# Relative-position attention with a mixture of experts: rows of maxima in one transfer, near values loaded later, routing steps and two small blocks moved to other slots

## The chip, the cores and the metric

The kernel runs on 1 core of one Trainium2 chip (trn2). The metric is device microseconds of one execution. Before: 1708.11 us, the median of 3 runs (1687.08 to 1716.86).

## The reference

x is [4, 1024, 128] in float32. The output is x + attention(xn) + ffn(xn), with xn the layer norm of x. The attention has 16 heads of 8 numbers, with a learned bias by distance (63 buckets, clipped at 31) on the queries and on the keys, and a term by distance on the values:

```python
attn = jnp.einsum('bhid,bhjd->bhij', q, k)                 # q scaled by hd ** -0.5
attn = attn + take_along_axis(einsum('bhid,hdm->bhim', q, rpe_k_table), idx)
attn = attn + swapaxes(take_along_axis(einsum('bhjd,hdm->bhjm', k * scale, rpe_q_table), idx), 2, 3)
attn = jax.nn.softmax(attn, axis=-1)
out = jnp.einsum('bhij,bhjd->bhid', attn, v)
S = segment_sum(attn over j, by bucket of i and j)         # 63 sums for each i
out = out + jnp.einsum('inbh,hnd->bhid', S, rpe_v_table)
x_out @ w_proj.T + b_proj
```

The ffn is a routed one (64 experts, the 6 best of a softmax for each of 4096 tokens, at most 64 tokens for an expert) beside a shared one.

## The kernel before

The attention is worked off head by head: 4 batches x 16 heads are 64 "heads", numbered 0 to 63. Each engine has its own hand-written program. They all run through iterations h, and an iteration has 16 slots s. In a slot TensorE makes two score tiles of 128 x 512, with small pieces around them:

- the first unit, of head h + 1, from Q1 and K1 (banks 0 and 1). VectorE reads it for the maxima of its rows (`tops`, line 1622). The bank is free again when VectorE has read it, so the first unit of slot s waits for the read of slot s - 2;
- the second unit, of head h - 1 in slots 0 to 5 and of head h from slot 6 on (LAG = 6), from Q2 and K2 (banks 2 and 3). Rows 8 to 10 of Q2 (ROW_M) hold the negated maxima in three bf16 parts, so that the scores come out with the maximum taken off, and ScalarE takes the exponential into PT (line 1277);
- in odd slots the product with the values; in slot 4 the query side of the distance bias for head h + 4 (copied by ScalarE into dq_e, line 1307, written to memory by SP, read back sheared as dq_s); in slot 7 its key side; in slot 13 the near values, a product of the windows WP with TOE. TOE depends on the attention head alone and is loaded by SP once for two heads (line 504), in odd iterations h (and once more after the experts).

Between the two passes over a head stand the maxima. VectorE folds `tops` into `top` (line 1603) in slot 0, TensorE transposes it in slot 1 (line 981), VectorE reduces the result and cuts it into three bf16 parts (lines 1611 to 1618, on 32 partitions, with a semaphore behind each operation), and SP copies the parts into the three rows of Q2, one transfer for a row (line 512). TensorE asks for them at slot 6, with `own(mrow_in, 48 * (h + 1))` (line 887).

SP's order in an iteration: TOE (if due), the maxima, rows of Q1 and K1 for head h + 2, dq_d, rows of Q2 and K2 for h + 1, operands of slots 4 and 7, the source of the windows (aj_d), and dq_s. All of these are issued from one queue. ScalarE issues the loads of the windows WT from its own queue, in slots 1, 5, 9 and 13. In slot 4 it copies a finished output of head h - 2 out of a bank (Oev, line 1332).

The routing for the experts runs on VectorE beside the heads: `routing(h)` gives q, j = divmod(h + 3, 7) for q < 4, and in the iterations with j of 3 to 6 (16 of them, heads 0 to 24) four "listing" steps find the best tokens of an expert one after another (`dve.max` on 576 columns, line 1537, and `match_replace`, line 1539). After head 29 the experts are computed, then the loop goes on with heads 30 to 63.

## Time and profile before

| | |
|---|---|
| median of 3 runs | 1708.11 us |
| profiled execution | 1702.14 us, span 1700.3 us |
| TensorE busy | 1428.5 us (84%) |
| VectorE busy | 1140.3 us (67%) |
| ScalarE busy | 797.6 us (47%) |
| GpSimd busy | 542.0 us (32%) |
| mean granted clock of TensorE | 0.864 |
| DMA | 289.55 MB, 170 GB/s |

The chain that ended last has TensorE for 52% of the span, VectorE for 23%, DMA for 8% and SP's queue for 6%. The page gives, for each group of instructions, the busy time and the idle time of its engine just before it with what ended that; the same can be asked for any stretch of time. The profile writes SPq for instructions of SP's queue, and x3 for three of a kind in a row.

### The profile page before, as it was taken

How to read it: one execution, taken by the hardware profiler on the slowest of the kernel's cores; microseconds unless marked ns; L12 is line 12 of the kernel's file. 1: busy time of each engine (PE TensorE's matmuls, PEld its weight loads, DVE VectorE, ACT ScalarE, POOL GpSimd, SP SyncE). 2: the span in 40 equal slices, each digit the busy share in tenths (PEclk: the TensorE clock that was granted, in tenths of full speed). 3: DMA queues.
4: the chain of work that ended last, by engine and by line, in shares of the span. 5: the costliest groups of instructions: out<-in, count | busy, mean ns of one | idle time of the engine just before them, and what ended most of it. 6: DMA issues, size and time to landing. Idle time of an engine off the chain costs nothing.

```text
span 1700.3 us, 67734 instructions
## 1 busy us (share of the span) xinstructions
PE 1428.5 (84%) x29626; PEld 963.5 (57%) x29626; DVE 1140.3 (67%) x2468; ACT 797.6 (47%) x1408; POOL 542.0 (32%) x555
## 2 busy tenths in 40 slices
PE   3376498888988989888889998989988888898897
PEld 1233255555655556555558666666656665666665
DVE  7275467878787786867653466777766666656672
ACT  2133134555455454544442255555545554545454
POOL 2244212222222222211333133444433333433343
PEclk9788558999799797977985589999989997979799
DMA  3665655776566565555555467667757665666553
GB/s 87 134 171 148 178 177 168 214 216 199 151 193 201 159 180 172 161 150 158 173 177 147 133 178 192 189 186 205 201 164 198 177 185 165 182 172 186 151 140 93
DMA packets 264392, 289.55 MB, mean 170 GB/s; under 512 B 45289, under 2 KB 195938, under 8 KB 264272
## 3 DMA queue, kind: packets, MB, share of 16 engines
q1 hardware_dynamic: 150400, 230.92, 45.0%
q10 hardware_dynamic: 102400, 50.35, 12.4%
q0 software_dynamic: 11472, 6.83, 2.8%
q8 instruction: 57, 0.93, 0.2%
q14 instruction: 63, 0.52, 0.1%
HBM read 173.84 MB, written 116.43 MB: 171 GB/s over the span
## 4 chain that ended last, share of the span: by engine, by line
PE 52%; DVE 23%; DMA 8%; SPq 6%; issue 5%; DVEq 2%; ACT 2%; POOL 1%; ACTq 1%; another core or an unknown queue 0%; POOLq 0%
PE PS L727 45%; DVE tops L1622 12%; DMA Q<-mparts 6%; PE PS L1086 5%; DVE dq_s L1648 3%; SPq L512 1%; SPq L432 1%; SPq L399 1%; DVE top L1603 1%; DVEq L1601 1%; ACT PT L1277 1%; DVE KT L1539 1%; DVE Ym L1653 1%; PE PS L1074 1%; DMA dq_s<-dq_d 1%
## 5 line engine op out<-in xcount | busy, mean ns | idle before, releaser
L1622 DVE TRANSPOSE_TENSOR_REDUCE tops<-PS 128x16 f32<-128x512 f32 x1024 | 699.7, 702 | 301.9 <-PE PS L727 295.7
L727 PE MATMUL PS<-Q,K 65*32 65x512 bf16 (+26 forms) x11904 | 722.7, 340 | 142.8 <-DVE tops L1622 73.8
L1277 ACT ACTIVATE PT<-PS 128x512 f32<-128x512 f32 x1024 | 594.6, 598 | 523.4 <-PE PS L727 470.8
L727 PEld LDWEIGHTS PS<-Q,K 65*32 65x32 bf16 (+1 forms) x11904 | 335.3, 102 | 354.7 <-DVE tops L1622 125.0
L668 POOL COPY WP<-PT 128x768 f32<-128x768 f32 x128 | 105.3, 823 | 841.5 <-PE PS L727 827.4
L727 PE MATMUL PS<-PT,Vst 128*9 128x256 f32 (+7 forms) x7552 | 366.8, 302 | 0.5 <-ACT PT L1277 0.5
L727 PE MATMUL PS<-WT,eye 96*32 96x96 bf16 (+2 forms) x4352 | 302.4, 213 | 4.6 <-DMA WT<-aj_d 3.3
L727 PEld LDWEIGHTS PS<-PT,Vst 128*9 128x9 f32 x7552 | 185.0, 95 | 72.6 <-issue 28.6
L727 PEld LDWEIGHTS PS<-WT,eye 96*32 96x32 bf16 x4352 | 190.4, 103 | 31.7 <-issue 7.2
L687 POOL TENSOR_TENSOR ajp<-dq_s,ajp 128x508 bf16<-128x508 f32 x128 | 148.8, 1163 | 10.4
L1312 ACT ACTIVATE ajp<-PS 128x508 bf16<-128x508 f32 x128 | 76.7, 599 | 88.1 <-PE PS L727 88.1
L685 POOL CAST ajp<-dq_s 128x508 bf16<-128x508 f32 x128 | 81.6, 637 | 111.5 <-DVE dq_s L1648 111.5
L727 PE MATMUL PS<-WP,TOE 128*64 128x64 f32 (+1 forms) x3072 | 115.2, 237 | 1.5 <-issue 1.5
L727 PEld LDWEIGHTS PS<-WP,TOE 128*64 128x64 f32 x3072 | 106.1, 150 | 18.2 <-issue 18.2
L656 POOL DMA_INDIRECT acc_d<-XNA,tok_i x64 | 100.8, 1575 | 42.8 <-DMA acc_d<-XNA,tok_i 36.5
L1086 PE MATMUL PS<-ident,dq_s 127*128 127x127 f32 x512 | 101.8, 333 | 14.7 <-DMA dq_s<-dq_d 14.7
L1307 ACT ACTIVATE dq_e<-PS 128x1024 f32<-128x1024 f32 x64 | 65.5, 1023 | 87.9 <-PE PS L727 87.9
L1648 DVE TENSOR_TENSOR dq_s<-PS,ajp 128x508 f32<-128x508 f32 x128 | 83.2, 650 | 28.1 <-ACT ajp L1312 28.1
L1653 DVE TENSOR_TENSOR Ym<-PS,ymask 128x512 f32<-128x512 f32 x64 | 44.3, 691 | 79.0 <-PE PS L727 70.3
L727 PE MATMUL PS<-PT,WT 128*88 128x512 f32 (+2 forms) x128 | 55.8, 630 | 44.8 <-ACT TOE L1234 29.5
L1086 PEld LDWEIGHTS PS<-ident,dq_s 127*128 127x128 f32 x512 | 68.7, 171 | 34.3 <-issue 34.3
L727 PE MATMUL PS<-tabk,Ka 71*128 71x127 bf16 x512 | 61.9, 256 | 0.0
(205 smaller groups left out, 1056.4 us busy)
## 6 DMA issues: line engine op xcount, KB each, us to landing
aj_d<-ajp SPq DMA_DIRECT2D x256, 192.0 KB
WT<-aj_d ACTq DMA_DIRECT2D x256, 192.0 KB, 3.0
dq_d<-dq_e SPq DMA_DIRECT2D x64, 512.0 KB, 4.0
dq_s<-dq_d SPq DMA_DIRECT2D x64, 512.0 KB
TOE<-toe_d SPq DMA_DIRECT2D x33, 768.0 KB
Q<-q_img SPq DMA_DIRECT2D x128, 120.0 KB, 2.6
K<-k_img SPq DMA_DIRECT2D x128, 120.0 KB, 2.7
q_img<-PT SPq DMA_DIRECT2D x48, 128.0 KB, 2.4
```

Source lines behind the costliest of these rows:

```text
L656: pool.indirect_dma_start(out=acc_d, out_offset=bass.IndirectOffsetOnAxis(ap=tok_i[:, 1 + half, n:n + 1], axis=0), in_=Y[:, n, :], in_offs ...
L668: pool.tensor_copy(WP[:, 4 * part:4 * part + 4, :], src).then_inc(win_in[part], 1)
L685: pool.tensor_copy(low[:, 0], r1).then_inc(aj_mid, 1)
L687: pool.tensor_tensor(low[:, 1], r1, low[:, 0], ALU.subtract).then_inc(aj_parts, 1)
L727: return pe.matmul(o, l, r, start=start, stop=stop, skip_group_check=True)
L1086: pe.matmul(PS[:, bank, a * P:a * P + DIST], dq_s[0:DIST, J * P:(J + 1) * P], ident[0:DIST, 0:DIST], start=a == 0, stop=False, is_transpos ...
L1277: act.activation(PT[:, TILE + N * J + 512 * half:TILE + N * J + 512 * half + 512], PS[:, 2 + u % 2, :], ACT.Exp).then_inc(s2_read, 1)
L1307: act.activation(dq_e[:, :], MISC, ACT.Copy).then_inc(dq_copied, 1)
L1312: act.activation(ajp[:, 0, 4 * part:4 * part + 4, 0:DIST], PS[:, 6 + part, :].rearrange("p (a n) -> p a n", n=P)[:, :, 0:DIST], ACT.Copy). ...
L1622: dve.tensor_reduce(tops[:, (h + 1) % 2, s // 2, 16 * (s % 2):16 * (s % 2) + 16], PS[:, s % 2, :].rearrange("p (c i) -> p c i", i=TILE), A ...
L1648: dve.tensor_tensor(dst, src, ajp[:, 0, 4 * part:4 * part + 4, 0:DIST], ALU.subtract).then_inc(aj_copied, 1)
L1653: dve.tensor_tensor(Ym[:, :].rearrange("p (m x) -> p m x", x=8), PS[:, 6, :].rearrange("p (m x) -> p m x", x=8), ymask[:, :].unsqueeze(1). ...
```

## The change

It has five parts.

1. The three parts of the maxima lie on 96 partitions, one below another (`mparts`, [3 x 32, 32]), and go into the three rows of Q2 in one transfer. Its semaphore counts 16 where it counted 48.
2. On SP the load of TOE stands behind the maxima and the rows of Q1 and K1, where it stood first.
3. On VectorE the operations on the maxima stand behind slot 1's tile, and are five where they were six: two reductions of the same columns (float32 and bf16), and three subtractions. One semaphore wait stands among them where there were four.
4. On ScalarE, Oev is copied in slot 2, where it was slot 4.
5. The listing steps stand in slots 3, 5, 6 and 7, where they stood in 5, 10, 12 and 15.

```diff
+LISTING = (3, 5, 6, 7)
...
-        mx = sb("mx", [TILE, 3, TILE])
-        mparts = sb("mparts", [TILE, 3, TILE], BF16)
+        mx = sb("mx", [2 * TILE, TILE])
+        mparts = sb("mparts", [3 * TILE, TILE], BF16)
...
                 on = lambda n: (not peeled) or 0 <= c + n < HEADS
+                if h == hm:
+                    load_distances(h + 3)
+                if on(0):
+
+                    sp.wait_ge(mparts_ready, h + 1)
+                    sp.dma_start(Q2[ROW_M:ROW_M + 3, h % PAIR, :].rearrange("p (c j) -> p c j", j=TILE),
+                                 mparts[:, :]).then_inc(mrow_in, 16)
+                if on(2):
+                    if h + 1 >= 0:
+                        sp.wait_ge(s1_ready, SLOTS * (h + 1) + 1)
+                    load_rows(h + 2, Q1, K1, rows1_in)
                 if on(-1) and fresh(h - 1):
                     wait(sp, y_psum, h - 1)
                     own = toe_d[bass.ds(place(h - 1)[1], 1), 0:SPAN, :].rearrange("a v d -> a (v d)")
                     sp.dma_start(TOE[:, :, :].rearrange("p a b -> p (a b)"),
                                  rows(own, own.offset, [[HD, P], [1, SPAN * HD]])).then_inc(toe_in, 16)
-                if h == hm:
-                    load_distances(h + 3)
-                if on(0):
-
-                    sp.wait_ge(mparts_ready, h + 1)
-                    for n in range(3):
-                        sp.dma_start(Q2[ROW_M + n:ROW_M + n + 1, h % PAIR, :].rearrange("p (c j) -> p c j", j=TILE),
-                                     mparts[:, n, :]).then_inc(mrow_in, 16)
-                if on(2):
-                    if h + 1 >= 0:
-                        sp.wait_ge(s1_ready, SLOTS * (h + 1) + 1)
-                    load_rows(h + 2, Q1, K1, rows1_in)
...
-                    own(mrow_in, 48 * (h + 1))
+                    own(mrow_in, 16 * (h + 1))
...
-                    if s == 4 and on(-2):
+                    if s == 2 and on(-2):
                         act.wait_ge(rel_done, h - 1)
                         act.wait_ge(fin_psum, h - 1)
...
-                if s in (5, 10, 12, 15) and 3 <= j:
-                    r, replace = divmod(4 * (j - 3) + (5, 10, 12, 15).index(s), 2)
+                if s in LISTING and 3 <= j:
+                    r, replace = divmod(4 * (j - 3) + LISTING.index(s), 2)
...
-                    if s == 1 and on(0):
-
-                        def hstep(ins, m):
-                            ins.then_inc(max_step, 1)
-                            dve.wait_ge(max_step, 4 * h + m)
-                        dve.wait_ge(top_psum, h + 1)
-                        wait(dve, s2_ready, SLOTS * (h - 1) + 1)
-                        dve.tensor_reduce(mx[:, 0, :], PS[0:TILE, 6, 0:P].rearrange("p (g j) -> p j g", g=4), AX.X, ALU.max,
-                                          negate=True).then_inc(top_read, 1)
-                        dve.drain()
-                        hstep(dve.tensor_copy(mparts[:, 0, :], mx[:, 0, :]), 1)
-                        hstep(dve.tensor_tensor(mx[:, 1, :], mx[:, 0, :], mparts[:, 0, :], ALU.subtract), 2)
-                        hstep(dve.tensor_copy(mparts[:, 1, :], mx[:, 1, :]), 3)
-                        hstep(dve.tensor_tensor(mx[:, 2, :], mx[:, 1, :], mparts[:, 1, :], ALU.subtract), 4)
-                        dve.tensor_copy(mparts[:, 2, :], mx[:, 2, :]).then_inc(mparts_ready, 1)
                     if on(1):
 
                         dve.wait_ge(s1_ready, SLOTS * (h + 1) + s + 1)
                         dve.tensor_reduce(tops[:, (h + 1) % 2, s // 2, 16 * (s % 2):16 * (s % 2) + 16],
                                           PS[:, s % 2, :].rearrange("p (c i) -> p c i", i=TILE), AX.X, ALU.max,
                                           apply_transpose=True).then_inc(s1_read, 1)
+                    if s == 1 and on(0):
+
+                        whole, rest = slice(0, TILE), slice(TILE, 2 * TILE)
+                        columns = PS[0:TILE, 6, 0:P].rearrange("p (g j) -> p j g", g=4)
+                        dve.wait_ge(top_psum, h + 1)
+                        wait(dve, s2_ready, SLOTS * (h - 1) + 1)
+                        dve.tensor_reduce(mx[whole, :], columns, AX.X, ALU.max, negate=True)
+                        dve.tensor_reduce(mparts[whole, :], columns, AX.X, ALU.max, negate=True).then_inc(top_read, 1)
+                        dve.drain()
+                        dve.tensor_tensor(mx[rest, :], mx[whole, :], mparts[whole, :], ALU.subtract)
+                        dve.tensor_tensor(mparts[rest, :], mx[whole, :], mparts[whole, :], ALU.subtract).then_inc(max_step, 1)
+                        dve.wait_ge(max_step, h + 1)
+                        dve.tensor_tensor(mparts[2 * TILE:3 * TILE, :], mx[rest, :], mparts[rest, :],
+                                          ALU.subtract).then_inc(mparts_ready, 1)
```

The instructions in SP's queue around the maxima, in the odd iteration h = 7 (TOE due), before:

```order
L553 DMA aj_d<-ajp 32x3x1024 x4
L493 DMA dq_s<-dq_d 128x1024
L504 DMA TOE<-toe_d 128x1536
L512 DMA Q2<-mparts 1x32x32 x3
L470 DMA Q1<-q_img 60x1024
L471 DMA K1<-k_img 60x1024
L521 DMA dq_d<-dq_e 128x1024
```

And now:

```order
L553 DMA aj_d<-ajp 32x3x1024 x4
L494 DMA dq_s<-dq_d 128x1024
L507 DMA Q2<-mparts 3x32x32
L471 DMA Q1<-q_img 60x1024
L472 DMA K1<-k_img 60x1024
L516 DMA TOE<-toe_d 128x1536
L521 DMA dq_d<-dq_e 128x1024
```

TOE has moved past three rows, and the maxima are one instruction.

On VectorE, the first half of iteration h = 8, one with listing steps (L1603 is `top`, slot 0; L1622 is a tile's read, L1607 in the kernel after; L1537 and L1539 are listing steps), before:

```order
L1603 TENSOR_REDUCE top<-tops 128x32
L1622 TENSOR_REDUCE tops<-PS 128x16
L1611 TENSOR_REDUCE mx<-PS 32x32
L1614 CAST mparts<-mx 32x32
L1615 TENSOR_TENSOR mx<-mx,mparts 32x32
L1616 CAST mparts<-mx 32x32
L1617 TENSOR_TENSOR mx<-mx,mparts 32x32
L1618 CAST mparts<-mx 32x32
L1622 TENSOR_REDUCE tops<-PS 128x16 x4
L1631 TENSOR_TENSOR Vst<-VR,TV 128x16x8
L1622 TENSOR_REDUCE tops<-PS 128x16
L1537 MAX lists<-KT 128x8
```

And now:

```order
L1603 TENSOR_REDUCE top<-tops 128x32
L1607 TENSOR_REDUCE tops<-PS 128x16 x2
L1616 TENSOR_REDUCE mx<-PS 32x32
L1617 TENSOR_REDUCE mparts<-PS 32x32
L1619 TENSOR_TENSOR mx<-mx,mparts 32x32
L1620 TENSOR_TENSOR mparts<-mx,mparts 32x32
L1622 TENSOR_TENSOR mparts<-mx,mparts 32x32
L1607 TENSOR_REDUCE tops<-PS 128x16 x2
L1537 MAX lists<-KT 128x8
L1607 TENSOR_REDUCE tops<-PS 128x16
L1630 TENSOR_TENSOR Vst<-VR,TV 128x16x8
L1607 TENSOR_REDUCE tops<-PS 128x16
```

Slot 1's tile stands ahead of the operations on the maxima, and the first listing step has come to slot 3.

The end of the same iteration, from slot 12's tile to the next `top`, before:

```order
L1622 TENSOR_REDUCE tops<-PS 128x16
L1537 MAX lists<-KT 128x8
L1622 TENSOR_REDUCE tops<-PS 128x16
L1653 TENSOR_TENSOR Ym<-PS,ymask 128x512
L1622 TENSOR_REDUCE tops<-PS 128x16 x2
L1539 MATCH_REPLACE KT<-lists,KT 128x576
L1603 TENSOR_REDUCE top<-tops 128x32
```

And now, from slot 11's small operations on:

```order
L1636 RECIPROCAL rden<-PS 128x8
L1640 TENSOR_TENSOR VR<-PS,rden 128x8x8
L1607 TENSOR_REDUCE tops<-PS 128x16 x2
L1652 TENSOR_TENSOR Ym<-PS,ymask 128x512
L1607 TENSOR_REDUCE tops<-PS 128x16 x2
L1603 TENSOR_REDUCE top<-tops 128x32
```

The two listing steps of slots 12 and 15 are gone from there.

## Rows read from the trace of the kernel before

**Rows 1.** The page's part 2: TensorE's granted clock in 40 slices of the span.

```profile
PEclk9788558999799797977985589999989997979799
```

**Rows 2.** Stretches: start:end length, busy us of PE, PEld, DVE, ACT, POOL; clock.

```profile
990.46:1608.45 617.99, 551.58 (x13033) 385.11 (x13026) 420.00 (x841) 328.52 (x581) 239.48 (x232) 0.92 0.66 184
...
1111.82:1133.94 22.12, 19.14 (x458) 13.42 (x452) 14.39 (x29) 11.34 (x20) 8.26 (x8) 0.92 0.67 193
1133.94:1153.09 19.15, 17.68 (x460) 12.48 (x454) 14.35 (x29) 11.21 (x20) 8.26 (x8) 1.00 0.67 179
1230.38:1256.82 26.44, 23.15 (x456) 15.03 (x452) 14.93 (x29) 11.57 (x20) 8.25 (x8) 0.74 0.69 192
```

**Rows 3.** TensorE's waits (us, times, longest): 990.46 to 1608.45, then 720 to 870.

```profile
PE PS L727 <- DMA Q<-mparts: 30.5, 14, 3.2
...
PE PS L727 <- DMA Q<-mparts: 7.2, 2, 4.4
```

**Rows 4.** The page's part 6: DMA issues, KB each, median us to landing.

```profile
TOE<-toe_d SPq DMA_DIRECT2D x33, 768.0 KB
Q<-q_img SPq DMA_DIRECT2D x128, 120.0 KB, 2.6
```

**Rows 5.** SP's timeline (start us, us) in heads 37 and 38.

```profile
1111.85 0.61 SPq L504 DMA_DIRECT2D TOE<-toe_d  x1
1114.34 1.79 SPq L512 DMA_DIRECT2D Q<-mparts  x3
...
1136.47 1.78 SPq L512 DMA_DIRECT2D Q<-mparts  x3
```

**Rows 6.** TensorE's timeline, [idle before]: head 38, slots 3 and 6; head 37.

```profile
1137.12 0.62 PE L727 MATMUL PS<-Q,K 65*32 65x512 bf16 x12 [0.69 <-DVE tops L1622]
1140.94 0.41 PE L727 MATMUL PS<-Q,K 65*32 65x512 bf16 x6 [0.39 <-ACT PT L1277]
...
1120.60 0.41 PE L727 MATMUL PS<-Q,K 65*32 65x512 bf16 x6 [2.11 <-DMA Q<-mparts]
```

**Rows 7.** VectorE's timeline at the start of head 38.

```profile
1135.11 0.24 DVE L1611 TENSOR_REDUCE mx<-PS 32x32 f32<-32x128 f32 x1
...
1136.28 0.17 DVE L1618 CAST mparts<-mx 32x32 bf16<-32x32 f32 x1
1136.37 1.92 DVE L1622 TRANSPOSE_TENSOR_REDUCE tops<-PS 128x16 f32<-128x512 f32 x3
```

**Rows 8.** ScalarE's timeline, slots 3 to 5 of head 38.

```profile
1138.05 0.60 ACT L1277 ACTIVATE PT<-PS 128x512 f32<-128x512 f32 x1 [0.97 <-PE PS L727]
1139.29 1.02 ACT L1307 ACTIVATE dq_e<-PS 128x1024 f32<-128x1024 f32 x1 [0.64 <-PE PS L727]
...
1140.68 0.39 ACT L1332 ACTIVATE Oev<-PS 128x256 f32<-128x256 f32 x1
```

**Rows 9.** SP's timeline in the preparation: two issues in a row.

```profile
31.15 0.28 SPq L429 DMA_DIRECT2D toe_d<-Ym  x1
31.47 22.23 SPq L432 DMA_DIRECT2D dq_d<-PT  x1
```

**Rows 10.** Head 8: a listing step; TensorE's waits for tile 11, for `top`.

```profile
411.82 0.74 DVE L1539 MATCH_REPLACE8 KT<-lists,KT 128x576 f32<-128x576 f32 x1
...
407.46 0.41 PE L727 MATMUL PS<-Q,K 71*32 71x224 bf16 x8 [0.57 <-DVE tops L1622]
...
413.31 0.29 PE L981 MATMUL PS<-ident,top 128*32 128x128 f32 x1 [0.73 <-DVE top L1603]
```

**Rows 11.** VectorE's waits in head 38, 1136 to 1145 us.

```profile
DVE tops L1622 <- PE PS L727: 3.0, 5, 1.9
```

**Rows 12.** Stretches, as in rows 2: head 8; head 10; heads 23 to 28.

```profile
392.47:412.66 20.19, 17.45 (x449) 11.79 (x449) 17.23 (x36) 11.37 (x21) 5.12 (x7) 1.00 0.62 176
...
432.84:461.20 28.36, 27.01 (x435) 17.40 (x439) 17.05 (x35) 11.64 (x20) 4.68 (x6) 0.58 0.55 162
...
720.57:869.89 149.32, 129.27 (x2698) 84.02 (x2698) 98.64 (x217) 69.31 (x122) 36.70 (x43) 0.82 0.55 159
```

More of the change, by code:

```diff
@@ L1029, in iteration @@
                         if s == 14:
-                            take(ins, mrow_in, 48)
+                            take(ins, mrow_in, 16)
                         if s == 15:
@@ L1150, in pairs @@
                     assert each == {s1_read.name: 2 * SLOTS, s2_read.name: 2 * SLOTS, rows1_in.name: 2 * ROWS_IN,
-                                    rows2_in.name: 2 * ROWS_IN, mrow_in.name: 96, v_ready.name: 2, o_copied.name: 2,
+                                    rows2_in.name: 2 * ROWS_IN, mrow_in.name: 32, v_ready.name: 2, o_copied.name: 2,
                                     top_ready.name: 2, top_read.name: 2, on_ready.name: 2, ym_ready.name: 2,
```

## The prediction, made before the changed kernel was run

> **What bounds the kernel now.** I read the page first. The profiled execution took 1702.14 us, its span is 1700.3, so 1.8 us lie outside; the median of the runs shown, 1708.11, is 0.35% above it, and the runs themselves lie 30 us apart. TensorE's granted clock is not full: many of the 40 slices stand at 5 to 9 tenths [rows 1]. So I asked for stretches, cut at each head's `top` reduction (T below is its start), to see which heads are slow.
>
> In the steady part, 990.46 to 1608.45 us, 29 heads take 617.99 us [rows 2]. Head 38 takes 19.15 us at clock 1.00, head 37 takes 22.12 at 0.92, head 43 takes 26.44 at 0.74: 0.50 stands for 1.2 GHz, 1.00 for 2.4. The odd iterations are slow, and these are the ones in which SP loads the near values TOE. At 19.15 each the 29 heads would take 555.4 us; 62.6 us are excess.
>
> The waits say what it is: in this part TensorE waited 14 times, 30.5 us in all, for the rows of maxima (DMA Q<-mparts) [rows 3]. SP's timeline shows why: in head 37 the 768 KB of TOE [rows 4] are issued at 1111.85, 2.5 us before the maxima's three transfers at 1114.34 [rows 5]. TensorE goes on at 1120.60, 6.3 us after that issue, after 2.11 us idle; in head 38, without TOE, the issue is at 1136.47 and the same unit starts at 1140.94, held for 0.39 us by an exponential only [rows 5, 6]. So there the maxima had landed within 4.5 us. The rest of the excess (62.6 less 30.5) is mostly TensorE's slower clock after the idle stretch: 0.92 or 0.74 over such a head.
>
> A clean head still has three waits of TensorE: 0.69 us at T+3.2 for VectorE's read of slot 1's tile, 0.39 at T+7.0 for ScalarE, and a third at T+12 that the change leaves. The first two are shown [rows 6]. VectorE's timeline explains the first: behind `top` and slot 0's tile it works on the maxima from 1135.11 (mx) until 1136.45, and only then reads slot 1's tile [rows 7]. ScalarE's explains the second: dq_e (1.02 us) and Oev (0.39) stand around one exponential, just where slot 6 waits [rows 8].
>
> **The change part by part.**
>
> (a) The queue. TOE goes behind the maxima and behind the rows of Q1 and K1. Nothing of 768 KB stands before the maxima any more in an odd head. In time: the clean heads' transfer lands before slot 6 asks. Excess removed: between 30.5 us (the idle alone, should the clock stay as it is) and 62.6; I take 60. What TOE is moved past must be counted: behind it now stand dq_d and the rows of Q2 and K2, which are asked for in the next head, and TOE itself is asked for at slot 12, some 10 us after its new issue (about T+5; in head 37 it went out at T+0.0). Its cover is those 10 us against the 6.3 us in which TOE and maxima together landed in head 37, and if that cover goes, slot 12 waits.
>
> (b) One transfer instead of three. The three issues take 1.79 us of SP, about 0.6 each [rows 5], and the last piece can only start then. One issue: 1.2 us less from `mparts` to landing.
>
> The trace bounds what one transfer with three rows on one side costs. A transfer with 127 on the outside (toe_d<-Ym, 127x16 pieces of 32 bytes) was issued at 31.15, and the next one kept SP for 22.23 us [rows 9]: it had to wait until a ring had drained 2032 pieces one after another, 11 ns each. The worst for 96 pieces, all one after another, is then 1.05 us; the best is what three transfers of 32 have, next to nothing. I take 0.35 (32 in turn on each of three). Net: 0.85 us earlier, bounds 0.15 and 1.2.
>
> The Trainium skill, "DMA: Bandwidth & Descriptors", section "Why a DMA increments its semaphore by 16 and not by 1", speaks against this part: a transfer from SP is spread over the largest number up to 16 of engines that divides the outermost size on both sides, so three rows would use three engines where 32 used sixteen. The 22.23 us above agree with it for 127. By it the 0.35 us stand; without it they would be near zero, and the sum is the same.
>
> (c) Five operations behind slot 1's tile. Before: from mx at 1135.11 to the last at 1136.45, 1.34 us. After: tile 1 first. It is ready when TensorE ends it, about T+1.3, and its read takes 0.63 to 0.71, so it ends at T+2.0 instead of T+3.1. Then two reductions of 0.24 (the second is new), the drain, three subtractions of 0.18, one wait: 0.24+0.24+0.09+0.18+0.18+0.04+0.18 = 1.15. `mparts` comes at T+3.1 instead of T+2.5: 0.6 later, less than the 0.85 won in (b). TensorE no longer waits at slot 3; it does at slot 4, for tile 2, whose read now begins behind the five operations and ends near T+3.7. TensorE, from T+2.5 (1137.12 less 0.69) plus 0.85 for slot 3, is there at T+3.35: it waits 0.35. Won: 0.34 per head, bounds 0 (the wait is only moved) and 0.69.
>
> (d) Oev from slot 4 to slot 2 on ScalarE. There ScalarE idles 0.97 us before its next exponential [rows 8], which hides its 0.39 us; at slot 4 it no longer stands before the awaited exponentials. Won: 0.39 at most, 0 if dq_e alone holds them; I take 0.2. What it copies was complete a head earlier.
>
> (c) and (d) bring 0.54 us in each of about 60 heads: 32 us, bounds 0 and 65. Do the maxima still come in time? No row has their landing. The nearest is that of the 120 KB of Q rows, 2.6 us from issue to landing [rows 4]. By it the last of three landed by T+6.3, and slot 6 asked at T+6.6. Now: issue at T+3.1, plus 2.6, plus the 0.35 of (b), is T+6.05, and slot 6 asks at T+6.1. It is just enough, with what ScalarE still holds slot 6 behind it. With 1.05 instead of 0.35 each head waits 0.5 more, 30 us in all; I take nothing and keep that for the range.
>
> (e) Listing steps. Each is about 0.74 us on VectorE, four in 16 of the heads 0 to 24. Before, in head 8, the one of slot 10 puts tile 11's read off, and TensorE waits 0.57 us for it; the one of slot 15 puts `top` off, and TensorE waits 0.73 [rows 10], against under 0.4 where head 38 has no such step. Slots 3 to 7 have room: in head 38 VectorE waits five times for TensorE between T+2 and T+11, 3.0 us in all, the longest 1.9 [rows 11], for 2.9 us of steps. Head 8 takes 20.19 us [rows 12], a clean head later on 19.15. Won: 0.9 in each of some 14 heads at full clock, 12 us; bounds 0 (they now hold slots 5 to 8) and 16.
>
> (f) Slow clock in the early part. Head 10 takes 28.36 us at clock 0.58, against head 8's 20.19 [rows 12], and two more of the heads 3 to 22 are like it: 25 us. TensorE waited for no maxima in it; before its clock fell, 3 us into the head, it had only the waits that (c) and (e) shrink, for `top` and for tile 1. Between 0 and 25; I take 9, one of the three.
>
> (g) Heads 23 to 28 take 149.32 us [rows 12] where 20.19 each is 121.1. Two of them waited 7.2 us for maxima, with slow clock behind it [rows 3]. Between 7 and 28; I take 12.
>
> Sum: 60 + 32 + 12 + 9 + 12 = 125 us. 1702 - 125 = 1577, and the same for the median within the runs' own spread; rounded to 1575.
>
> **The rivals.**
>
> R1, only the queue order counts. The wait for tile 1 comes back whole as one for tile 2, dq_e alone holds the exponentials, and steps at 5, 6, 7 in a row hold tiles. For it: VectorE has as many tiles as before, and its reads are back to back from slot 8 to 12. Against: its idle time at slots 3 to 7. Then (c), (d), (e) and (f) give nothing: 1702 - 60 - 12 = 1630.
>
> R2, the clock. Faster heads meet the dips elsewhere: (f) gives nothing and three or four more heads of the loop fall to half clock, at 7 us each (26.44 less 19.15). For it: head 10 fell without any wait for maxima. Against: no head of the loop fell that had not waited for maxima. 1577 + 9 + 25 = 1611.
>
> R3, TOE only changes its victim. Behind the rows it meets ScalarE's window loads and dq_d, and slot 8 or 12 waits in odd heads, half of the excess staying: 1577 + 30 = 1607.
>
> R4, slower. The one transfer with few pieces in flight lands late in every head, not in odd ones alone, and slot 6 waits each time with the clock falling behind it. The 14 waiting heads of the loop took (617.99 - 15 x 19.2) / 14 = 23.6 us. If all 29 do, and the 30 early ones lose the same 4.4: 29 x 4.4 + 30 x 4.4 - 62.6 = 197 more, less 32 for (c) and (d): 1867. A wait begins with a landing 3.0 us after issue; for this price it must be over 2 us long, a landing 5.2 us after issue. Above the Q rows' 2.6 that is 2.6 us for 96 pieces, 27 ns each in one line, more than twice the row's 11.
>
> **How the numbers follow.** Forecast 0.60, with its own range 1545 to 1602; R1 0.16; R2 0.13; R3 0.06; R4 0.03; the remaining 0.02 is no change. About 2% (34 us) is what a measurement of this kernel can tell from no change. All but R4 and the last lie more than 2% below 1708: faster 0.94, within 2% 0.03, slower 0.03. The range for 8 in 10 takes the forecast's low end and reaches up to R1: 1543 to 1630.
>
> **What would show it.** Right: no wait for Q<-mparts in the loop; odd and even heads alike, near 18.6 us, clock 1.00; the waits at T+3 and T+7 gone or halved, one of about 0.35 near T+3.5; one issue of about 0.6 us in place of 1.79; in head 8 no 0.57 at T+15 (slot 13). Wrong: a wait for mparts in even heads too (R4), a wait of 0.7 for tile 2 (R1), heads at 0.6 to 0.9 clock without a DMA wait (R2), a wait for TOE or WT at slots 8 to 12 (R3).

## The result, and the profile after

| | before | changed |
|---|---|---|
| runs, median (range) | 1701.19 us (1687.08 to 1716.86, 4 runs) | 1545.11 us (1531.95 to 1557.28, 4 runs) |
| ratio, 95% interval | | 0.9082 (0.8946 to 0.9217) |
| profiled execution, span | 1702.14, 1700.3 | 1552.42, 1550.6 |
| granted clock, mean | 0.864 | 0.911 |
| heads 3 to 22 | 429.01 | 392.42 |
| heads 23 to 28 | 149.32 | 130.04 |
| heads 31 to 59 | 617.99 | 531.90 |

(The median of before has one run more in it than the one shown ahead.) The change makes the kernel 9.2% faster. Forecast was 1575 us, 30 more than the median; the result lies 2 us above the low end of the range (1543), and the second measurement of the same kernel (e9) gave 1537.86, just under it: that the median fell inside is in part luck. A ratio compares means and leaves out executions more than 1.5% above a kernel's fastest, so it is not quite the quotient of the medians.

The page of the changed kernel, the clock and the line of VectorE's tile reads:

```profile
PEclk9869557799999999998898579999999999999999
...
L1607 DVE TRANSPOSE_TENSOR_REDUCE tops<-PS 128x16 f32<-128x512 f32 x1024 | 700.0, 703 | 170.0 <-PE PS L727 148.7
```

Set beside [rows 1]: from the 25th slice on the clock stands at 9 (90% or more). Stretches, cut as before at the `top` reductions (start:end length, then busy us of PE, PEld, DVE, ACT, POOL, the clock, DMA share, GB/s):

```profile
927.70:1459.60 531.90, 495.96 (x13031) 343.01 (x13025) 420.01 (x812) 327.30 (x580) 239.52 (x232) 1.00 0.81 214
1056.54:1074.85 18.31, 17.08 (x460) 11.85 (x453) 14.47 (x29) 11.27 (x20) 8.26 (x8) 1.00 0.69 191
1038.19:1056.54 18.35, 17.08 (x459) 11.83 (x453) 14.52 (x29) 11.29 (x20) 8.25 (x8) 1.00 0.88 233
390.73:409.36 18.63, 17.32 (x460) 11.72 (x453) 17.11 (x35) 11.26 (x20) 5.13 (x6) 1.00 0.67 192
...
686.47:816.51 130.04, 115.60 (x2708) 78.36 (x2702) 98.95 (x212) 68.72 (x122) 37.05 (x42) 0.90 0.66 182
```

These are heads 31 to 59, head 38, head 37, head 8 and heads 23 to 28, against [rows 2, 12]. Head 37, with near values, takes what head 38 takes; the clock of all 29 is 1.00 where it was 0.92. VectorE's work in them is the same, 420 us.

TensorE's waits in heads 31 to 59 (us, times, longest), and then in heads 3 to 28:

```profile
PE PS L727 <- DVE tops L1607: 23.6, 58, 0.5
PE PS L727 <- ACT PT L1277: 11.3, 29, 0.4
...
PE PS L727 <- DVE tops L1607: 30.4, 60, 1.6
PE PS L727 <- ACT PT L1277: 8.1, 23, 0.4
PE PS L727 <- DMA Q<-mparts: 5.4, 3, 1.9
```

The 14 waits for the maxima, 30.5 us [rows 3], are gone from the loop; three are left, in heads 17, 23 and 25. Waits for tiles and for ScalarE are still there, two and one in each head. Their place is seen in head 38, TensorE's timeline:

```profile
1060.39 0.40 PE L727 MATMUL PS<-Q,K 71*32 71x224 bf16 x8 [0.43 <-DVE tops L1607]
1063.29 0.41 PE L727 MATMUL PS<-Q,K 65*32 65x512 bf16 x6 [0.39 <-ACT PT L1277]
1068.49 0.40 PE L727 MATMUL PS<-Q,K 71*32 71x96 bf16 x8 [0.37 <-DVE tops L1607]
```

T is 1056.54 here. The wait of 0.69 for tile 1 [rows 6] became one of 0.43 for tile 2, at T+3.85; the one for ScalarE at slot 6 has kept its 0.39. VectorE and SP at the start of this head:

```profile
1057.09 1.53 DVE L1607 TRANSPOSE_TENSOR_REDUCE tops<-PS 128x16 f32<-128x512 f32 x2
1058.55 0.24 DVE L1616 TENSOR_REDUCE mx<-PS 32x32 f32<-32x128 f32 x1
...
1059.40 0.18 DVE L1622 TENSOR_TENSOR mparts<-mx,mparts 32x32 bf16<-32x32 f32 x1
1059.61 1.99 DVE L1607 TRANSPOSE_TENSOR_REDUCE tops<-PS 128x16 f32<-128x512 f32 x3
```

```profile
1059.61 0.73 SPq L507 DMA_DIRECT2D Q<-mparts  x1
1060.39 0.48 SPq L471 DMA_DIRECT2D Q<-q_img  x1
```

Tile 1 is read ahead of the maxima, the last of the three parts ends at T+3.04 (before at T+2.5), and one issue of 0.73 us stands where three took 1.79 [rows 5, 7].

The waits alone don't tell what a head won. Better is the time between the ends of TensorE's first units of two slots, from the trace, for head 38, from slot 1 on: before 0.98, 1.31, 0.98, 1.09, 0.95, 1.10, 2.65, 0.53, 0.87, 1.09, 1.36, 0.52, 3.01; changed 0.98, 0.44, 1.59, 1.09, 0.95, 1.10, 2.48, 0.53, 0.87, 1.09, 1.36, 0.52, 2.55. Three places differ: slots 2 to 4 together (0.26 us won), slots 7 to 8 (0.17), and slots 13 to 14 (0.46), which the prediction had not foreseen. The experiments have to say of each what it belongs to.

### The profile page after: what moved, and what is told of

Same layout as the page of the kernel before. It is cut to its first block, busy times and chain, and to the rows that moved or that the text cites. A ratio compares the mean times of both kernels' runs of the same rounds, so it can differ in the third digit from the quotient of the medians.

```text
span 1550.6 us, 67554 instructions
## 1 busy us (share of the span) xinstructions
PE 1330.6 (86%) x29626; PEld 905.3 (58%) x29626; DVE 1139.0 (73%) x2404; ACT 793.3 (51%) x1408; POOL 541.9 (35%) x555
## 4 chain that ended last, share of the span: by engine, by line
PE 58%; DVE 21%; SPq 5%; DMA 5%; issue 4%; DVEq 3%; ACT 2%; POOL 1%; ACTq 1%; POOLq 0%
PE PS L727 51%; DVE tops L1607 11%; PE PS L1086 4%; DVEq L1618 3%; DVE dq_s L1647 3%; ACT PT L1277 2%; SPq L433 1%; SPq L400 1%; PE PS L1074 1%; PE PS L981 1%; DMA dq_s<-dq_d 1%; DMA Q<-mparts 1%; ACTq L1296 1%; SPq L445 1%; DVE KT L1539 1%
## 5 line engine op out<-in xcount | busy, mean ns | idle before, releaser
L1607 DVE TRANSPOSE_TENSOR_REDUCE tops<-PS 128x16 f32<-128x512 f32 x1024 | 700.0, 703 | 170.0 <-PE PS L727 148.7
L727 PE MATMUL PS<-Q,K 65*32 65x512 bf16 (+28 forms) x11904 | 654.9, 325 | 98.9 <-DVE tops L1607 63.3
L727 PEld LDWEIGHTS PS<-Q,K 65*32 65x32 bf16 (+1 forms) x11904 | 307.8, 99 | 290.0 <-DVE tops L1607 110.2
L727 PE MATMUL PS<-PT,Vst 128*9 128x256 f32 (+7 forms) x7552 | 327.1, 289 | 0.9 <-issue 0.6
L727 PE MATMUL PS<-WT,eye 96*32 96x96 bf16 (+2 forms) x4352 | 281.7, 208 | 3.6 <-DMA WT<-aj_d 3.3
L727 PEld LDWEIGHTS PS<-PT,Vst 128*9 128x9 f32 x7552 | 168.7, 92 | 60.5 <-issue 14.1
L727 PEld LDWEIGHTS PS<-WT,eye 96*32 96x32 bf16 x4352 | 173.4, 100 | 29.9 <-DMA WT<-aj_d 4.1
L727 PE MATMUL PS<-WP,TOE 128*64 128x64 f32 (+1 forms) x3072 | 110.4, 232 | 1.0 <-issue 1.0
L1086 PE MATMUL PS<-ident,dq_s 127*128 127x127 f32 x512 | 87.7, 298 | 14.7 <-DMA dq_s<-dq_d 14.7
L1086 PEld LDWEIGHTS PS<-ident,dq_s 127*128 127x128 f32 x512 | 58.8, 152 | 32.2 <-issue 32.2
L727 PEld LDWEIGHTS PS<-PT,WT 128*88 128x88 f32 (+2 forms) x128 | 17.0, 162 | 71.2 <-issue 35.1
```

Source lines behind the costliest of these rows:

```text
L727: return pe.matmul(o, l, r, start=start, stop=stop, skip_group_check=True)
L1086: pe.matmul(PS[:, bank, a * P:a * P + DIST], dq_s[0:DIST, J * P:(J + 1) * P], ident[0:DIST, 0:DIST], start=a == 0, stop=False, is_transpos ...
L1607: dve.tensor_reduce(tops[:, (h + 1) % 2, s // 2, 16 * (s % 2):16 * (s % 2) + 16], PS[:, s % 2, :].rearrange("p (c i) -> p c i", i=TILE), A ...
```

## The experiments

Each group of kernels ran on one chip, with the kernel before beside it; the first four (e1 to e4) had one chip, e5 to e8 a second, e9 and e10 a third, e11 and e12 a fourth. The kernel before took 1709.88, 1696.82, 1691.92 and 1688.73 us there (median of 7 runs each), so ratios are compared, or stretches. The executions of one kernel on one chip lie up to 49 us apart, so small differences are read from the heads and not from the totals.

**e1, the queue order alone.** The kernel before, and in SP's iteration:

```diff
-                if on(-1) and fresh(h - 1):
-                    ...
-                    sp.dma_start(TOE[:, :, :].rearrange("p a b -> p (a b)"),
...
                     load_rows(h + 2, Q1, K1, rows1_in)
+                if on(-1) and fresh(h - 1):
+                    ...
+                    sp.dma_start(TOE[:, :, :].rearrange("p a b -> p (a b)"),
```

> The kernel before, with one part of the change: TOE behind the maxima and the rows of Q1 and K1. Theory Q (the wait for maxima came from TOE alone, and the slow clock behind it too): the odd heads of the loop take what the even ones took, 19.15 us, at clock 1.00, no wait for Q<-mparts there; 29 x 19.15 = 555 us instead of 618, in all some 60 to 75 us less than before, 1625 to 1640. Rival S (the single transfer or the earlier tile read is needed as well for the maxima to land in time): odd heads keep a wait of 0.5 us or more and dips of the clock; 1650 to 1690.

Measured: 1619.20 us (1606.69 to 1630.02, 4 runs), ratio 0.9507 (0.9404 to 0.9609), 90.7 us of medians. Heads 31 to 59:

```profile
960.59:1518.87 558.28, 512.54 (x13031) 359.88 (x13024) 417.53 (x841) 324.72 (x580) 239.91 (x232) 1.00 0.79 204
```

59.7 us less than before, all clock 1.00, and none of the waits for maxima in them. Heads 3 to 22 gained 14.2 us, heads 23 to 28 10.0. One moved block is more than half of the whole result. In these heads it gives back the idle time (30.5 us) and about as much again (29.2 us), as the clock of the stretch rose from 0.92 to 1.00.

**e2, everything but the queue order.** The changed kernel with the same block moved back:

```diff
+                if on(-1) and fresh(h - 1):
+                    ...
                 if h == hm:
                     load_distances(h + 3)
...
-                if on(-1) and fresh(h - 1):
-                    ...
```

> The kernel after, with TOE first in SP's queue again. Theory Q: odd heads wait for the maxima again, 2 to 3 us, as TOE stands before them whatever the number of transfers; the clock dips again; 60 to 85 us slower than the kernel after, 1605 to 1630; even heads keep 18.3. Rival S (one transfer suffices): waits under 1 us, under 25 us slower.

Measured: 1640.77 us (1622.23 to 1652.38, 4 runs), ratio 0.9652 (0.9566 to 0.9739). In heads 31 to 59:

```profile
PE PS L727 <- DMA Q<-mparts: 20.7, 14, 2.8
```

14 waits as before, two thirds as long: a shorter transfer behind 768 KB is still behind 768 KB. The time lies 11 us above what was expected (1605 to 1630); the waits came as theory Q has them.

**e3, the five operations ahead of tile 1.**

```diff
-                    if on(1):
-                        ...
-                        dve.tensor_reduce(tops[:, (h + 1) % 2, s // 2, 16 * (s % 2):16 * (s % 2) + 16],
                     if s == 1 and on(0):
                         ...
+                    if on(1):
+                        ...
+                        dve.tensor_reduce(tops[:, (h + 1) % 2, s // 2, 16 * (s % 2):16 * (s % 2) + 16],
```

> The kernel after, with the five operations on the maxima ahead of slot 1's tile again. From the intervals between TensorE's units (before 0.98, 1.31, 0.98; after 0.98, 0.44, 1.59) the move is worth 0.26 us a head: 18.3 becomes 18.5 to 18.6 in the loop, some 15 us in all (1560). The wait at slot 3 is back at 0.4 to 0.7, for five operations are shorter than six. Rival: the move is worth nothing and the fewer operations everything: 18.3 stays.

Measured: 1564.32 us (1558.63 to 1570.00, 2 runs), ratio 0.9181 (0.9078 to 0.9284). Slots 1 to 4 of head 39: 0.98, 1.14, 0.97, in sum 3.09 where the changed kernel has 3.01 and the kernel before 3.27. So of the 0.26 us only 0.08 are the order. The other 0.18 lie between the kernel before and e3, which have the operations at the same place, six and five of them. VectorE's timeline bears it out: in head 39 of e3, which starts at 1080.82, the read of tile 1 begins at T+2.22, and before it began at T+2.43 [rows 7].

```profile
1083.04 1.94 DVE L1621 TRANSPOSE_TENSOR_REDUCE tops<-PS 128x16 f32<-128x512 f32 x3
```

Head 39 was chosen because other heads of e3 are disturbed in these slots by the pause of the last section. In a listing head this kernel was even 0.18 us quicker:

```profile
383.72:402.17 18.45, 17.07 (x459) 11.79 (x453) 17.01 (x34) 11.38 (x20) 5.13 (x6) 1.00 0.68 192
```

**e4, three transfers.** The changed kernel with

```diff
-                    sp.dma_start(Q2[ROW_M:ROW_M + 3, h % PAIR, :].rearrange("p (c j) -> p c j", j=TILE),
-                                 mparts[:, :]).then_inc(mrow_in, 16)
+                    for n in range(3):
+                        sp.dma_start(Q2[ROW_M + n:ROW_M + n + 1, h % PAIR, :].rearrange("p (c j) -> p c j", j=TILE),
+                                     mparts[TILE * n:TILE * n + TILE, :]).then_inc(mrow_in, 16)
```

and the counts 48 and 96 in TensorE's waits.

> The kernel after, with three transfers for the rows of maxima (semaphore 48 again). Mine: they start 0.6 us later than before the change and end 1.2 us later than one transfer would, so slot 6 waits 0.2 to 0.8 us for Q<-mparts in every head, the period 18.5 to 19.1 us, 1555 to 1600 in all. Rival: the landing has slack, period 18.3, no wait, same time as after. Second question: the interval between the units of slots 13 and 14 in the loop behind the experts was 3.01 us before and is 2.55 after; if the semaphore's count of 48 instead of 16 makes it, it is 3.01 here.

Measured: 1584.64 us (1582.77 to 1586.51, 2 runs), ratio 0.9300 (0.9206 to 0.9395). TensorE's waits in heads 31 to 59:

```profile
PE PS L728 <- DMA WT<-aj_d: 6.0, 6, 1.9
...
PE PS L728 <- DMA Q<-mparts: 0.8, 2, 0.4
```

A wait in every head had been expected, and there is none: the maxima come in time, except in a few heads (0, 17, 23, 25, 60, 62 waited 0.6 to 2.6 us; the last part of the program took 101.6 us instead of 91.0). From the packet records, median of heads 30 to 59: start of the issue to the last of the 96 pieces 2.60 us with three transfers, 2.03 with one; to the last raise of the semaphore 2.99 and 2.37 us (heads 31 to 59). Beside that TensorE waits six times for the windows (WT). In these heads it did so not at all in the changed kernel, and in the other kernels with one transfer 0 to 3 times (none in e7 and e8, 2.9 us in e11, which has the most), so that the six come of the three transfers is likely but not shown by this one profile.

**e5, Oev at slot 4.**

```diff
-                    if s == 2 and on(-2):
+                    if s == 4 and on(-2):
```

> The changed kernel with the copy of Oev back at slot 4 of the head (it stands at slot 2). In the changed kernel the ends of TensorE's first units of slots 7 and 8 lie 2.48 us apart, before 2.65; slots 13 to 14 in the heads behind the experts 2.55, before 3.01. Theory A (the copy is worth 0.17 us in a head, at slot 7): the first interval is 2.65 again, the rest of the head as in the changed kernel, heads 31 to 59 of 18.5 us, the time 11 us over the changed kernel's. Theory B (the place of the copy is what shortens slot 13 to 14 too): that interval is 3.01 again as well, heads of 18.95 us, the time 25 to 30 us over. Theory C (the prediction's place): slot 6 to 7 changes by 0.2 and slot 7 to 8 by nothing.

Measured: 1573.22 us (1569.95 to 1576.49, 2 runs), ratio 0.9268 (0.9180 to 0.9355). Slots 7 to 8 take 2.65 again. The prediction had put the gain at slot 6; that wait is 0.39 before and after. Against e7, which has the same heads behind the experts and ran on the same chip, heads 31 to 59 are 553.53 to 546.77: 0.23 us a head.

**e6, the listing steps spread as before.**

```diff
-LISTING = (3, 5, 6, 7)
+LISTING = (5, 10, 12, 15)
```

> The changed kernel with the routing steps of the listing heads at slots 5, 10, 12, 15 as before (they stand at 3, 5, 6, 7). Theory A (the steps are 0.9 us a listing head, 14 heads in heads 3 to 22): listing heads of 19.5 to 19.7 us where the changed kernel has 18.6, the time 12 to 16 us over the changed kernel's. Theory B (the steps' place also decides where TensorE's clock falls): beside that one or two more heads of heads 3 to 22 at 27 to 29 us, the time 20 to 35 us over. Theory C (the steps lie beside other work): heads of 18.6, no difference. In no theory does a head behind the experts change: 18.3 us, slots 13 to 14 2.55 us apart; if that is 3.05 there, the interval follows something else than the edit.

Measured: 1575.45 us (1572.45 to 1578.45, 2 runs), ratio 0.9281 (0.9194 to 0.9368). Head 8:

```profile
392.49:412.24 19.75, 17.27 (x449) 11.90 (x449) 17.29 (x34) 11.37 (x21) 5.13 (x7) 1.00 0.63 178
```

19.75 for 18.63: 1.1 us a listing head. Theory A held; of theory B nothing shows (no head between 7 and 19 fell to a low clock).

e5 and e6 also showed 3.05 us for slots 13 to 14, as e1 to e4 had, although e6 changes nothing in the heads behind the experts. More on that at e9.

**e7, expert weights behind the maxima.** In SP's iteration, behind the TOE load:

```diff
+                if h in (14, 17):
+                    ...
+                    load_w13(sp, {14: 1, 17: 2}[h])
+                    load_w2(sp, {14: 1, 17: 2}[h])
...
-                if h in (13, 16):
-                    ...
-                    load_w13(sp, {13: 1, 16: 2}[h])
-                    load_w2(sp, {13: 1, 16: 2}[h])
```

and in the same way from `h == 22` to 23 and from `h == 24` to 25.

> The changed kernel with SyncE's four issues of expert weights moved by half a head: they stand behind the maxima and the near values of heads 14, 17, 23 and 25, where the changed kernel has them at the end of heads 13, 16, 22 and 24, ahead of the next head's maxima. Theory A (the three waits for the maxima that are left, 1.95, 1.74 and 1.71 us in heads 17, 23 and 25, are the maxima's small transfer behind the weights in the queue): the three waits vanish; 5.4 us gained from the waits alone, 10 to 17 with the fallen clock behind them (heads 17, 23, 25 of 22.5, 26.9, 24.8 us at 19 to 20). Theory B (the waits go but the clock falls anyway, by the weights' own load or in another head): 0 to 6 us gained. Theory C (the weights come too late for the experts, or collide with heads' own loads): slower by 3 to 20 us, and the first expert waits for WT or w13.

Measured: 1555.58 us (1548.22 to 1559.22, 5 runs), ratio 0.9178 (0.9114 to 0.9242). Heads 3 to 22 and 23 to 28:

```profile
288.23:673.18 384.95, 349.11 (x9002) 238.66 (x8996) 336.45 (x720) 229.73 (x406) 106.33 (x120) 1.00 0.73 206
673.18:794.35 121.17, 107.68 (x2718) 73.83 (x2708) 98.10 (x212) 68.11 (x122) 37.16 (x43) 0.99 0.71 198
```

No wait for the maxima is left anywhere, and heads 17, 23 and 25 take 18.3, 18.6 and 20.9 us (22.5, 26.9, 24.8 before this edit): theory A in these heads, 7.5 and 8.9 us in the two stretches. But head 30 took 28.8 us where it had 20.0, because the low clock that begins in the experts' part lasted almost to its end (836.9 to 908.6 us; the head runs from 881.2 to 909.9), and in total time nothing is shown to be won by this edit alone.

**e8, e7 with early steps in the two heads behind a listing one.**

```diff
-                if (j, s) == (1, 5):
+                if (j, s) == (1, 3):
-                if (j, s) == (1, 10):
+                if (j, s) == (1, 5):
-                if j == 1 and s in (12, 15):
+                if j == 1 and s in (6, 7):
-                if j == 2 and s in (5, 8):
+                if j == 2 and s in (5, 6):
-                if (j, s) == (2, 10):
+                if (j, s) == (2, 7):
```

> The kernel with the expert weights behind the maxima, and the routing steps of the other heads of each group of seven too at early slots: those of the first head behind a listing one at slots 3, 5, 6, 7 (were 5, 10, 12, 15), of the second at 5, 6, 7 (were 5, 8, 10). Theory A (a step behind slot 8 costs TensorE as in the listing heads): two heads of seven are shorter by 0.3 to 1.0 us each, six heads, 2 to 6 us under the kernel without this edit. Theory B (the steps' own work was hidden there): no difference. Theory C (DVE has no room for them at slots 3 to 7 of these heads): waits of TensorE for P or S at slots 4 to 8, slower by 1 to 5 us.

Measured: 1538.58 us (1537.66 to 1548.58, 4 runs), ratio 0.9083 (0.9012 to 0.9155), 17 us under e7 on the same chip. Heads 5, 12 and 19 take 18.3 us for 19.6, heads 6, 13 and 20 18.9 for 20.3 to 21.8; that is 9.6 us in six heads, more than was expected, of which heads 3 to 22 in sum keep 6.3, since head 17 took 21.2 us here. The two profiled executions lie 10.6 us apart. Heads 2 and 30 were 9.1 us shorter here, and heads 23 to 28 6.2 us longer, each by how long the low clock lasted, which the edit does not touch.

**e9, the changed kernel once more**, because only it had 2.55 us at slots 13 to 14.

> The changed kernel once more, no line altered. In its first profile the ends of TensorE's first units of slots 13 and 14 in the heads behind the experts lie 2.55 us apart; in the kernel before and in seven variants, which share these instructions of TensorE, 3.01 to 3.06. Theory A (the 0.5 us belong to the execution and not to the change): 3.05 us here too, heads 31 to 59 of 18.8 us instead of 18.3, heads 31 to 59 in sum 545 to 547 instead of 532. Theory B (the change as a whole, no part of it alone, removes them, by where the program's instructions come to lie): 2.55 us again, the sum 532. By theory A the change itself is worth 0.4 us less in each of these heads, and the profiled time of the changed kernel is 12 to 15 us under what its other executions take.

Measured: 1537.86 us (1524.83 to 1544.89, 4 runs), ratio 0.9111 (0.8977 to 0.9245); 2.55 us again, heads 31 to 59 531.82. The 0.5 us is a pause of TensorE's weight loads amid the products of values in slot 13. Here is e7, then the changed kernel (PEld, idle before in brackets):

```profile
1058.52 0.21 PEld L727 LDWEIGHTS PS<-PT,Vst 128*9 128x9 f32 x11
1059.05 0.13 PEld L727 LDWEIGHTS PS<-PT,Vst 128*9 128x9 f32 x5 [0.32 <-issue]
```

```profile
1072.53 0.23 PEld L727 LDWEIGHTS PS<-PT,Vst 128*9 128x9 f32 x16
1072.80 0.50 PEld L727 LDWEIGHTS PS<-Q,K 71*32 71x32 bf16 x12
```

No other engine released it ("issue"). The page shows it in one line, whose last number is that idle time; before, e7, the changed kernel, e9:

```profile
L727 PEld LDWEIGHTS PS<-PT,Vst 128*9 128x9 f32 x7552 | 185.0, 95 | 72.6 <-issue 28.6
```

```profile
L727 PEld LDWEIGHTS PS<-PT,Vst 128*9 128x9 f32 x7552 | 178.1, 91 | 69.4 <-issue 27.0
```

```profile
L727 PEld LDWEIGHTS PS<-PT,Vst 128*9 128x9 f32 x7552 | 168.7, 92 | 60.5 <-issue 14.1
```

```profile
L727 PEld LDWEIGHTS PS<-PT,Vst 128*9 128x9 f32 x7552 | 168.6, 92 | 61.7 <-issue 15.4
```

**e10, the loop's register additions in slot 3.** The three steps stand at the end of slot 3, their starting values one step lower:

```diff
-                    if s == 13 and looped:
+                    if s == 3 and looped:
                         pe.reg_add(heads_done, heads_done, 1)
                         pe.reg_add(dq_turn, dq_turn, 1)
                         pe.reg_add(aj_turn, aj_turn, 2)
```

> The changed kernel with TensorE's three additions to its loop's registers at the end of slot 3, ahead of the unit that waits for VectorE's tile at T+3.85, where they stand in slot 13 between the near values' products and the values'. The pause of 322 ns in the middle of the values' products in slot 13, seen in the variants of 3.05 us, has 'issue' as its end: nothing that another engine did. Theory A (the sequencer runs late by the additions, and the products run dry): slots 13 to 14 of 2.3 to 2.55 us in every execution, heads 31 to 59 of 18.3 us, 0.5 us in each of 29 heads or 15 us under the changed kernel's second run if that has 3.05. Theory B (the pause is the supply of the instructions themselves, at a place of the stream): 3.05 us stay. Theory C (it only moves): slots 3 to 5 longer by 0.1 to 0.4 us.

Measured: 1546.93 us (1524.15 to 1561.54, 4 runs), beside e9's 1537.86 on the same chip; 2.55 us at slots 13 to 14, heads 31 to 59 532.82. The additions cost nothing there, but since e9 had no pause either, this did not put theory A to the test.

**e11, both edits of e8 and e10.** The two diffs above.

> The kernel with the expert weights behind the maxima and the early routing steps in all three heads of a group, and beside that TensorE's three additions to its loop's registers at the end of slot 3 instead of slot 13. The changed kernel has 2.55 us between slots 13 and 14 behind the experts in both of its profiles, and so has the one with the additions moved; this kernel without the move has 3.04. Theory A (the additions put the sequencer behind): 2.55 us, heads 31 to 59 of 18.3 us, 14 us under the kernel without the move, about 1525 us. Theory B (the pause has nothing to do with them): 3.04 us, heads of 18.8, the time the same as without the move within 5 us.

Measured: 1518.37 us (1516.10 to 1521.01, 4 runs), ratio 0.9001 (0.8942 to 0.9061). Slots 13 to 14 take 2.55 us, e8 had 3.04: theory A's number. It is no proof of it, for e12, which leaves the additions in slot 13, has 2.55 too.

**e12, the changed kernel with the steps of all three heads** (e8's diff alone, without e7's).

> The changed kernel with, on VectorE alone, the routing steps of the two heads behind a listing one at early slots (3, 5, 6, 7 and 5, 6, 7); SyncE's order as changed, three waits for the maxima in heads 17, 23, 25 stay. Expected from the profile of the kernel that has the weights moved too: heads 5, 12, 19 of 18.3 to 18.4 us where the changed kernel has 19.6, heads 6, 13, 20 of 18.9 instead of 20.3 and more, heads 3 to 22 in sum 384 to 388 instead of 389 to 392, the time 4 to 10 us under the changed kernel's. If the pause between slots 13 and 14 behind the experts is a matter of this one program, 3.05 us there and 14 us given back; if only some edits bring it, 2.55.

Measured: 1526.57 us (1514.21 to 1541.18, 4 runs), ratio 0.9030 (0.8957 to 0.9103), slots 13 to 14 2.55 us. Heads 5, 12 and 19 take 18.3 us, heads 6, 13 and 20 18.9, as expected; heads 3 to 22 are 387.14 for e9's 388.76, since here heads 14 and 17 waited for the maxima (1.68 and 2.04 us) and took 21.3 and 27.3 us. The profiled execution is the slowest of the four (1541.18 us).

Seen together: all eight profiles of the first two chips have the pause (issue 24.1 to 31.6 us on the line above), all four of the other two do not (12.7 to 15.5), whatever the edit, TensorE's own program being one and the same in e7, e8, e9 and e12. The kernel before was slower on the first two chips as well, by (1709.88 + 1696.82 - 1691.92 - 1688.73) / 2 = 13.0 us, and 29 heads of 0.46 us are 13.3; but 1696.82 and 1691.92 alone are 5 us apart, so this is a weak sign. So the pause most likely goes with the chip or the execution, not with a part of the change. It is not shown: no program was profiled on both kinds of chip, which would settle it. Why the pause is there is open, and so is whether before and changed were profiled on one chip. That the change itself makes some 9% does not hang on it: e9 and the kernel before on the same chip give 0.9111.

e11 is the fastest of all: 1518.37 against 1526.57 for e12 on the same chip, and a ratio of 0.9001 against the changed kernel's 0.9082 and 0.9111. In it heads 3 to 24 all take 18.3 to 19.8 us, and no head waits for the maxima.

## Why the prediction was right

It named the mechanism and its size fairly: 125 us forecast, 149.7 between the two profiled executions, of which some 13 to 15 are the pause that one profile has and the other has not.

| part of the program | forecast gain | between the profiles |
|---|---|---|
| heads 31 to 59 | 60 (a) + 29 x 0.54 = 75.7 | 86.1; against e7, which has the pause too, 71.2 |
| heads 3 to 22 | 12 (e) + 9 (f) + 20 x 0.54 = 31.8 | 36.6, and 40.3 to e9 |
| heads 23 to 28 | 12 (g) + 6 x 0.54 = 15.2 | 19.3, and 15.9 to e9 |
| all others | 5 x 0.54 = 2.7 | 7.7 |

(a) The queue: right. 60 us forecast, 59.7 in heads 31 to 59 of e1. That the prediction took nearly all of the 62.6 and not only the 30.5 of idle time was the choice that mattered, and it rested on reading the clock beside the waits. In the whole program the moved block is worth 90.7 us (67 to 102 by the ratio's interval); (a), (f) and (g), the terms it can reach, come to 81.

(b) One transfer: right in kind, smaller than forecast: 0.57 us to the last piece and 0.62 to the last raise of the semaphore (e4 against the changed kernel), where 0.85 was forecast. The issues end at T+3.8 for T+4.3; the one issue takes 0.73 us where about 0.6 was taken. The 0.35 us for 96 pieces were not seen as a delay: in head 39 all pieces ran between T+4.45 and T+4.71, in head 38 until T+5.22, other transfers' packets running beside them. The Trainium skill's count of engines (page "DMA: Bandwidth & Descriptors", section "Why a DMA increments its semaphore by 16 and not by 1") makes it three engines, for it takes the largest number up to 16 that divides the outermost size of both sides, here 3 and 96. The trace agrees: the semaphore of the maxima is raised four times for each transfer, in head 39 once at T+4.23, before any piece, and three times behind the pieces, at T+5.10, 5.11 and 5.12. In 64 heads that is 256 times, where in e4, with three transfers of one row for each head, it is raised 3038 times; and the 0.26 us of head 39 are 8 ns for each of 32 in turn, where the prediction took 11. The forecast landing was T+6.05; the last raise came at T+5.62 (median of heads 31 to 59), before the exponential lets slot 6 go on at T+6.75. The price of the pieces stayed below the 0.35 and hid in the slack.

(c) Tile 1 first: 0.34 us forecast, 0.26 measured, but only 0.08 of it is the order. The step that failed is the comparison of 1.34 us at the old place with 1.15 at the new: it did not ask what the shorter operations are worth where they stood. e3 shows 0.18. That the sum came near is luck as to its cause. The wait for tile 2 was put at 0.35 near T+3.35; it is 0.43 at T+3.85. `mparts` at T+3.1: 3.04.

(d) Oev: 0.2 forecast, 0.17 to 0.23 measured, at another place. Slot 6 still waits 0.39 for its exponential, though Oev no longer stands before it; ScalarE in head 38 starts dq_e when TensorE has written it, and the exponentials come behind:

```profile
1059.57 0.38 ACT L1332 ACTIVATE Oev<-PS 128x256 f32<-128x256 f32 x1
...
1061.63 1.02 ACT L1307 ACTIVATE dq_e<-PS 128x1024 f32<-128x1024 f32 x1 [1.19 <-PE PS L727]
...
1062.55 1.08 ACT L1277 ACTIVATE PT<-PS 128x512 f32<-128x512 f32 x2
```

At slot 6 this is the prediction's own lower bound, "0 if dq_e alone holds them". What Oev held up was the exponential behind it, for which the second unit of slot 7 waits. The weight loads of that unit show it, in head 38 of e5 and then of e7:

```profile
1072.79 0.10 PEld L727 LDWEIGHTS PS<-Q,K 65*32 65x32 bf16 x4 [0.29 <-ACT PT L1277]
...
1049.68 0.21 PEld L727 LDWEIGHTS PS<-Q,K 65*32 65x32 bf16 x4
```

(e) Listing steps: 0.9 a head forecast, 1.1 measured in e6 (head 8). Right.

(f), (g) The early clock: 9 and 12 us forecast; heads 3 to 22 rose from clock 0.92 to 0.97, heads 23 to 28 from 0.82 to 0.90. The falls of heads 10, 16, 24 and 28 went, those of 20, 23, 25 and 26 stayed (34 us at the low clock in them, where it was 55), and new ones came at 13 and 17. e7 adds what was overlooked: three of these heads (17, 23, 25) stand behind a wait for maxima that another large load ahead in SP's queue causes, the expert weights. The prediction had looked for TOE alone. So (f) came out near its size without its reason being shown: which of heads 3 to 22 fall differs from profile to profile.

R1 (only the queue order counts, 1630): no, e1 is 0.9507 and the changed kernel 0.9082 and 0.9111. R2: the clock did fall in other early heads, but in none of heads 31 to 59. R3: no wait for TOE at slots 8 to 12, but its mechanism is there, and small. On the page the windows land 4.7 us after their issue where they took 3.0, and dq_d 5.2 where it took 4.0; in the loop TensorE waited for windows for 0.6 us in e9, 1.4 in e10, 1.2 in e12 and 2.9 in e11, always in odd heads, the ones with TOE. R4: no head of the loop waited for the single transfer in the changed kernel's first profile. The margin is thin: in e9, e10 and e12 one head of the 29 did (heads 50, 47 and 37: 0.59, 0.67 and 0.39 us). The landing R4 needs, 5.2 us after the issue, never came; the median is 2.37.

Step by step, by the list of what would show it: odd and even heads alike (18.3 us, forecast 18.6) at clock 1.00, no wait for maxima in the loop (first profile), one issue of 0.73 us for 1.79, no wait at slot 13 of head 8; the one at T+7 was to be gone or halved and was not.

## What to carry to other kernels

In a queue that serves one engine, small transfers that are asked for soon go ahead of large ones that are asked for late; look at every large load in the queue, the rare ones too, and at what the moved load now stands beside. Where a wait stands next to a fallen clock, a moved transfer gives back both, here 59.7 us for 30.5 of idle time. Measure a head from one tile's end to the next: a wait's length tells neither what an edit won nor where, as slots 2 to 4 and slot 7 showed. And small differences of a profile are only the edit's when a second profile of the same kernel has them.

## What had not been expected of the hardware

The pause in slot 13: 0.32 us without a weight load, amid 16 products that wait for nothing, about 0.5 us in the head's length, in nearly each of heads 31 to 59 of nine profiles and in none of these heads in five. It is not in slot 13 alone. In each of the nine profiles TensorE stands idle behind nothing ("issue") 3 to 24 times in heads 31 to 59, mostly in slots 2 and 3, and in the five it never does. In head 38 of e3 the first unit of slot 3 starts late in this way (first row), and in head 38 of e7 the 16 products of slot 3 take 1.08 us where the changed kernel's take 0.61. Such a head is about 0.3 us longer (19.12 us in e7, where 18.75 is usual).

```profile
1064.61 0.62 PE L727 MATMUL PS<-Q,K 65*32 65x512 bf16 x12 [0.51 <-issue]
...
1044.96 1.08 PE L727 MATMUL PS<-PT,Vst 128*9 128x160 f32 x16
...
1059.34 0.61 PE L727 MATMUL PS<-PT,Vst 128*9 128x160 f32 x16
```

In the first loop, heads 7 to 9, where TensorE runs the same slots, no profile has it. Its cause is open: the register additions were not moved on a chip where the pause is present.

The clock fell in some heads behind no wait for a transfer: in head 26 of e8, 28.1 us long at clock 0.57, TensorE waited once, 1.3 us for `top` at the head's start. It falls at other heads in each kernel. So the time of heads 2 to 30 moves with an edit that has nothing to do with it. The two profiles of the changed kernel differ by 3.7 us in heads 3 to 22 and by 3.4, the other way, in heads 23 to 28, and head 30 took 20.0 us in one kernel and 28.8 in another. The totals of e7, e8 and e12 carry that.
